# A four-layer graph network on one core: the load rearranged, and layer 1's sums moved between the blocks of a scan

## The reference, cut to what matters

```
x = layernorm(x + L0(x))
#  L0: deg = max(sum(adj,1)+1, 1); h = (adj @ x + x)/deg
#      z = relu([x, h] @ W + b);  z / max(|z|, 1e-12)
x = layernorm(x + L1(x))
#  L1: tanh([x, t] @ W1 + b1) @ W2 + b2 + adj @ (x B') - deg * (x B')
x = layernorm(x + L2(x))
#  L2: w @ (x @ weight) + bias, where w[i,j] = adj[i,j] * 0.5^(number of
#      neighbours of row i right of j), kept for the last 100 neighbours
x = layernorm(x + L3(x))
#  L3: logmap(adj @ expmap(x)) @ kernel + bias
```

## Time and profile before

| what | value |
|---|---|
| median of 3 runs | 169.18 us (169.04 to 169.3) |
| the profiled execution | 167.48 us |
| its span in the profile | 165.2 us |
| PE busy | 128.9 us, 78% of the span |
| DVE busy | 107.6 us, 65% |
| ACT busy | 69.5 us, 42% |
| POOL busy | 42.8 us, 26% |
| moved from memory | 17.93 MB |

### The profile page before, as it was taken

The page is one execution under the profiler, slowest core; times in us unless marked ns, Lnnn a source line. Parts: engine busy times, 40 slices in busy tenths (PEclk is TensorE's granted clock), DMA queues, the critical chain, the costliest instruction groups (busy, mean ns, idle before and its releaser), DMA issues.

```text
span 165.2 us, 2074 instructions
## 1 busy us (share of the span) xinstructions
PE 128.9 (78%) x728; PEld 67.7 (41%) x728; DVE 107.6 (65%) x240; ACT 69.5 (42%) x138; POOL 42.8 (26%) x50
## 2 busy tenths in 40 slices
PE   0018869957998899899999899999999899992000
PEld 0007753511443245143533555677447644572000
DVE  0589987789999999995176110622623888538861
ACT  0034201448566666754378547512113320257440
POOL 0000000102430143114344000433412552713290
PEclk9999999999999999999999999999999999999755
DMA  6999999999999995000000000000000000000006
GB/s 131 257 304 350 318 300 354 272 206 287 346 347 255 289 215 124 0 0 0 4 0 0 0 0 0 4 0 0 0 4 0 0 2 0 0 4 0 0 0 127
DMA packets 13945, 18.59 MB, mean 112 GB/s; under 512 B 5360, under 2 KB 5616, under 8 KB 13936
## 3 DMA queue, kind: packets, MB, share of 16 engines
q1 hardware_dynamic: 7728, 9.68, 22.2%
q10 hardware_dynamic: 6208, 8.78, 19.2%
HBM read 17.93 MB, written 0.52 MB: 112 GB/s over the span
## 4 chain that ended last, share of the span: by engine, by line
PE 45%; DVE 25%; DMA 13%; POOL 5%; issue 4%; ACT 4%; POOLq 1%; ACTq 0%; DVEq 0%
PE psS L737 15%; DMA WT<-adj 10%; PE psN L737 5%; PE psC L737 5%; DVE AT L494 4%; DVE AT L495 4%; DMA X<-x 3%; PE psC L804 3%; PE psC L806 3%; PE psX L813 2%; POOL root L272 2%; POOL nroot L291 2%; ACT WT L365 2%; PE psX L763 1%; PE psH L783 1%
## 5 line engine op out<-in xcount | busy, mean ns | idle before, releaser
L365 ACT ACTIVATE WT<-psC 128x512 int16<-128x512 f32 x64 | 36.9, 596 | 13.0 <-PE psC L806 9.8
L737 PE MATMUL psS<-AT,XP 128*128 128x512 bf16 x128 | 35.0, 390 | 0.9 <-DVE XP L500 0.9
L272 POOL TENSOR_TENSOR root<-var,power 128x4 f32<-128x4 f32 (+1 forms) x16 | 18.7, 1170 | 44.2 <-DVE var L546 19.5
L804 PE MATMUL psC<-AT,cb 128*128 128x512 bf16 x56 | 21.4, 383 | 4.5 <-ACT WT L365 4.5
L806 PE MATMUL psC<-AT,cb 128*128 128x512 bf16 x64 | 24.2, 379 | 0.0
L737 PEld LDWEIGHTS psS<-AT,XP 128*128 128x128 f16 x128 | 11.9, 100 | 17.0 <-issue 3.7
L763 PE MATMUL psX<-cb,XP 128*128 128x128 bf16 x32 | 4.0, 264 | 12.7 <-DVE XP L632 11.9
L494 DVE STREAM_TRANSPOSE AT<-stage 128x1024 bf16<-128x1024 bf16 x10 | 13.2, 1318 | 0.8 <-DMA stage<-adj 0.7
L804 PEld LDWEIGHTS psC<-AT,cb 128*128 128x128 bf16 x56 | 5.6, 101 | 18.6 <-ACT WT L365 16.0
L495 DVE STREAM_TRANSPOSE AT<-stage 128x1024 bf16<-128x1024 bf16 x10 | 12.7, 1270 | 0.0
L285 POOL TENSOR_TENSOR XB<-X,weights 128x256 f32<-128x256 f32 x12 | 9.6, 808 | 9.6 <-DVE X L551 9.6
(11 more groups left out here) (143 smaller groups left out, 223.3 us busy)
## 6 DMA issues: line engine op xcount, KB each, us to landing
stage<-adj ACTq DMA_DIRECT2D x20, 256.0 KB, 11.3
stage<-adj SPq DMA_DIRECT2D x20, 256.0 KB, 12.3
WT<-adj SPq DMA_DIRECT2D x12, 256.0 KB, 14.7
WT<-adj ACTq DMA_DIRECT2D x12, 256.0 KB, 14.0
out<-X SPq DMA_DIRECT2D x6, 64.0 KB, 1.9
weights<-weights_packed SPq DMA_DIRECT2D x1, 353.5 KB, 15.8
X<-x SPq DMA_DIRECT2D x2, 128.0 KB, 3.1
X<-x ACTq DMA_DIRECT2D x2, 128.0 KB, 4.0
```

The costliest lines, as they stand in the source:

```text
L272: nc.gpsimd.tensor_tensor(root[:, e, 0:n], var[:, e, 0:n], power[:, 0:n, 0:NR], ALU.pow).then_inc(root_ready, 1)
L365: nc.scalar.activation(WT[:, e, chain_block(bank, k)], psC[bank][:], ACT.Relu).then_inc(chain_taken, 1)
L737: ins = nc.tensor.matmul(bank, XP[:, l % 2, c], matrix, start=(c == 0), stop=last)
L804: nc.tensor.matmul(acc, C("past"), AT[:, c + 1, e], start=False, stop=False, skip_group_check=True)
```

## The change

On the load side:
- SP and ScalarE issue piece 0 before X. ScalarE issues pieces 1 to 5 at once, and later pieces at other places of its queue.
- VectorE transposes piece 0 before it waits for X, and piece 1 before it waits for the maximum. The high part of X's split moves to ScalarE (`split_high`).
- The parts of Z get four banks (psN[0], psN[1], psS[1], psC[0]); ScalarE takes them out, POOL adds the bias (`add_bias`).
- Chunk 0 is counted and summed in two halves of 256 columns: the first after pieces 0 and 1, ahead of the own parts, the second after them.
- VectorE's order from piece 6 on is written out; the last three transposes stand together ahead of activate0(2), and the centring of the weights moves behind it.

On the layer 1 side:
- CHAIN_IN_SUMS becomes (0, 10, 27, 38), CHAIN_LOOP 46. Eight sum blocks of layer 1 stand between chain blocks 18 to 25; transpose and hidden of chunk 0 stand among blocks 35 to 37, those of chunk 1 among 40 to 42.
- The last 18 chain blocks go in pairs between the steps of layer 1's end. POOL's residual additions of layer 1 come later in its queue.

```diff
 # SP
+            first = WR["WB"][0]
+            load_lower(0)
             for q in range(NQ // 2):
                 sp.dma_start(X[QD * q:QD * (q + 1)], xd[q]).then_inc(x_loaded, 16)
             sp.dma_start(cb[:].bitcast(U16), cpack).then_inc(consts_loaded, 16)
-            load_lower(0)
 # POOL
+            def add_bias(e):
+                pool.wait_ge(z_taken, e + 1)
+                nc.gpsimd.tensor_tensor(Z[:, chunk(e)], Z[:, chunk(e)], per_feature(W("b0")), ALU.add
+                                        ).then_inc(z_biased, 1)
 # ScalarE
+            def split_high():
+                act.wait_ge(inverse_ready, 1)
+                nc.scalar.activation(XP[:, 0, :, 0:D], X[:], ACT.Copy, scale=xs[:, 4:5]).then_inc(high_ready, 1)
+            def take_z(e):
+                act.wait_ge(z_ready, e + 1)
+                nc.scalar.activation(Z[:, chunk(e)], z_bank(e)[:, 0:NR * D]..., ACT.Copy).then_inc(z_taken, 1)
+            load_upper(0)
             for q in range(NQ // 2, NQ):
                 act.dma_start(X[QD * q:QD * (q + 1)], xd[q]).then_inc(x_loaded, 16)
-            for m in range(NR):
+            for m in range(1, 6):
                 load_upper(m)
-            for e in range(NE):
-                take_xt(0, e)
-                load_upper(NR + e)
+            split_high()
+            take_xt(0, 0)
+            load_upper(6)
+            take_xt(0, 1)
+            load_upper(7)
+            take_z(0)
+            take_xt(0, 2)
+            load_upper(8)
+            take_z(1)
+            take_xt(0, 3)
+            load_upper(9)
+            take_z(2)
+            take_z(3)
+            load_upper(10)
...
 # VectorE
+            transposes(0)
             dve.wait_ge(x_loaded, 16 * NQ)
             nc.vector.tensor_reduce(xs[:, 0:1], ...).then_inc(xmax_ready, 1)
             step(nc.vector.tensor_reduce(xmean[:], X[:], AX_X, ALU.add))
+            transposes(1)
             dve.wait_ge(xmax_all, 1)
...
-            transposes(0)
+            nc.vector.reciprocal(xs[:, 4:5], xs[:, 3:4]).then_inc(inverse_ready, 1)
             nc.vector.scalar_tensor_tensor(XB[:], per_node(xmean[:]), -1.0 / D, X[:], ALU.mult, ALU.add)
+            dve.wait_ge(high_ready, 1)
+            ... low part ...
+            for m in range(2, 6):
+                transposes(m)
+            ... h_bias ...
+            take_degrees(0); transposes(6); activate0(0); transposes(7); combine0(0)
+            transposes(8); normalise(0, 0); transposes(9); take_degrees(1); transposes(10)
+            activate0(1); transposes(11); combine0(1); transposes(12); normalise(0, 1)
+            take_degrees(2); transposes(13); transposes(14); transposes(15); activate0(2)
+            ... centring of the weights ...
+            take_degrees(3); combine0(2); activate0(3); normalise(0, 2); combine0(3); normalise(0, 3)
 # TensorE
+            count_half(0)
             transpose_x(0, 0)
+            sum_half(0)
+            transpose_x(0, 1)
+            own_part(0)
+            transpose_x(0, 2)
+            own_part(1)
+            transpose_x(0, 3)
+            own_part(2)
+            own_part(3)
+            count_half(1)
+            sum_half(1)
...
+                for k, n in enumerate(chain_after_sums(e)):
                     chain(n)
+                    if e == 1 and 2 <= k < 10:
+                        sum_block(1, k % 2, (k - 2) // 2)
...
+            chain_pair(CHAIN_LOOP)
             transpose_x(1, 2)
             sums(1, 1, late)
             add_own(1, 1)
+            chain_pair(CHAIN_LOOP + 2)
             dense(1, 0)
+            chain_pair(CHAIN_LOOP + 4)
             hidden(2)
+            sums(1, 2, late); add_own(1, 2); chain_pair(52); dense(1, 1); chain_pair(54)
+            transpose_x(1, 3); chain_pair(56); dense(1, 2); chain_pair(58); hidden(3)
+            chain_pair(60); chain_pair(62); sums(1, 3, range(0, 4)); add_own(1, 3)
```

More of the change, by code:

```diff
@@ L411, in _ @@
                 if e >= 1 and e < 3:
-                    for n in range(CHAIN_IN_SUMS[e], NB * e):
+                    for n in chain_in_sums(e):
                         take_chain(n)
+                        if n == CHAIN_IN_SUMS[1] + 4:
+                            load_upper(14)
                 take_sum(0, e)
                 if e < 3:
-                    for n in range(NB * e, CHAIN_IN_SUMS[e + 1]):
+                    for n in chain_after_sums(e):
                         take_chain(n)
[L418 to L423, removed]
@@ L646, in _ @@
                                            ).then_inc(h_bias_ready, 1)
+            take_degrees(0)
+            transposes(6)
+            activate0(0)
+            transposes(7)
+            combine0(0)
+            transposes(8)
+            normalise(0, 0)
+            transposes(9)
+            take_degrees(1)
+            transposes(10)
+            activate0(1)
+            transposes(11)
+            combine0(1)
+            transposes(12)
+            normalise(0, 1)
+            take_degrees(2)
+            transposes(13)
+            transposes(14)
+            transposes(15)
+            activate0(2)
             bundle = W(CENTRED[0], CENTRED[-1]).rearrange("p (k f) -> p k f", f=D)
@@ L650, in _ @@
                                            bundle, ALU.mult, ALU.add).then_inc(centred, 1)
[L651 to L657, removed]
-                activate0(e)
-                transposes(NR * e + 7)
-                combine0(e)
-            normalise(0, NE - 2)
-            take_degrees(NE - 1)
-            activate0(NE - 1)
-            combine0(NE - 1)
-            normalise(0, NE - 1)
+            take_degrees(3)
+            combine0(2)
+            activate0(3)
+            normalise(0, 2)
+            combine0(3)
+            normalise(0, 3)
             add_residual(1, 0)
@@ L807, in chain, with chain_pair @@
                                  skip_group_check=(k > 0)).then_inc(chain_ready, 1)
+            def chain_pair(n):
+                chain(n)
+                chain(n + 1)
             def hidden(e):
@@ L893, in _ @@
                 chain(n)
-                k = n - CHAIN_IN_SUMS[e] - 2
-                if k == -1:
+                k = n - CHAIN_IN_SUMS[e]
+                if k == 1:
                     dense(0, e)
-                if 0 <= k < 8:
+                if k == 2:
+                    transpose_x(1, 1)
+                if k == 4:
+                    hidden(1)
+                if k < 4:
+                    sum_block(1, 0, NR + k)
                     sum_block(1, 1, NR + k)
-                if 8 <= k < 12:
-                    sum_block(1, 0, k)
+            for c in range(2 * NR):
+                sum_block(1, 2, c)
+            for o in range(3):
+                sums(1, o, range(2, 3))
             sums(1, 0, late)
             add_own(1, 0)
+            chain_pair(CHAIN_LOOP)
             transpose_x(1, 2)
@@ L905, in _ @@
             add_own(1, 1)
+            chain_pair(CHAIN_LOOP + 2)
             dense(1, 0)
+            chain_pair(CHAIN_LOOP + 4)
             hidden(2)
-            for n in range(CHAIN_LOOP, CHAIN_ALL):
-                chain(n)
-                k = 2 * (n - CHAIN_LOOP)
-                if k < 12:
-                    sum_block(1, 2, k)
-                    sum_block(1, 2, k + 1)
-            dense(1, 1)
-            transpose_x(1, 3)
             sums(1, 2, late)
             add_own(1, 2)
-            sums(1, 3, range(0, 2))
+            chain_pair(CHAIN_LOOP + 6)
+            dense(1, 1)
+            chain_pair(CHAIN_LOOP + 8)
+            transpose_x(1, 3)
+            chain_pair(CHAIN_LOOP + 10)
+            dense(1, 2)
+            chain_pair(CHAIN_LOOP + 12)
             hidden(3)
-            dense(1, 2)
-            sums(1, 3, range(2, 4))
+            chain_pair(CHAIN_LOOP + 14)
+            chain_pair(CHAIN_LOOP + 16)
+            sums(1, 3, range(0, 4))
             add_own(1, 3)
```

169 lines of the change are left out of this document (103 added, 66 removed).

## The result

The changed kernel takes **167.03 us** (median of 4 runs, 166.16 to 167.45) against 169.24 us for the kernel before beside it (4 runs, 169.04 to 170.88): ratio 0.989, 95% interval 0.984 to 0.994. It is faster by 2.2 us where 2.4 slower was forecast. A second set of 12 runs gave 166.99 us, ratio 0.988 (0.984 to 0.992). The ratios leave disturbed runs out, so they can differ a little from the quotient of the medians.

What follows compares the result with a forecast made beforehand. VectorE was taken to set the pace, or nearly, up to 73 us, then TensorE. Layer 1's end at 115.0 against 112.08, less 0.5, gave +2.4: 169.9 profiled, 171.6 us as median; own range 170.3 to 172.8, over all cases 165.9 to 173.0.

Steps and rivals of the forecast that it cites:

- the 0.5 taken off: End of the sum: 0.5 us subtracted for a possible clock rise within the second half of chunk 0's sums.
- The start: Load up to TensorE's first transpose of X: piece 1, landing at 15.0, delays it to 20.7 us from 11.94.
- the table load: ScalarE's 1.28 us load before the high part: taken as hidden; a rival had it or the queue cost 1.3, chance 0.10.
- The clock: TensorE from 20.7 us: half sums and own parts at the low clock, own parts ending at 33.0, degrees at 35.9.
- The wait at take_degrees(0): VectorE ahead of piece 6: stands 5.8 us for the degrees of chunk 0; piece 7 ends at 45.3.
- early-clock rival: Start of TensorE's work: clock rises at 24.8, all after piece 7 is 5.8 earlier, 166.3 us; chance 0.32.
- The middle: VectorE from piece 7 to piece 15: 28.7 us, to 74.0; TensorE waits for piece 15, moved sums cost nothing.
- The end of layer 1: TensorE after chunk 3 of layer 0, from 78.9 us: 31.24 - 0.6 + 3.7 + 1.8, ending at 115.0 against 112.08.
- The stalls at the chain: Layer 1's end: new TensorE waits for ScalarE, 0.5 after hidden(1) and 1.3 at the last pairs and sums(1,3).
- No wait any more: Layer 1's end: split of chunk 3 comes 15 us after piece 15, at 89, needed at 90.9; 0.6 taken off.
- leftover work: After chunk 3 of layer 0: 4 chain blocks, 4 sums, a transpose and a hidden more remain, 3.7 us.
- From trace to median: Final step: the median's 1.7 us above the profiled execution is carried over, 169.9 to 171.6 us.

Runs made afterwards that it cites:

- half_late: The changed kernel with the first half of chunk 0's sums moved behind the own parts: 171.6 us, ratio 1.017.
- the two issue-time kernels: The kernel before and the changed kernel, each issuing upper halves of pieces 8 to 15 at the other's places: 168.11 us (0.994) and 168.68 us (0.995).
- layer1_only: The kernel before with only the change's chain and layer 1 orders on TensorE and ScalarE, load as before: 174.95 us, ratio 1.026.
- before_warm: The kernel before with twelve unused matmuls of 512 columns ahead of the first transpose of X: 169.67 us, ratio 1.007.
- before_early: The kernel before with upper halves of pieces 8 to 15 issued at the changed kernel's places: 168.11 us, ratio 0.994.
- load_only: The changed kernel's load with its VectorE and POOL orders, layer 1's blocks where they were before: 171.14 us, ratio 1.018.

## Why the prediction was wrong

The forecast, 171.6 us, was 4.6 too long. 2.7 of that lies in the trace (169.9 against 167.19) and 1.9 in the step from the profiled execution to the median. In the trace chunk 3 was over 4.2 us before the forecast, the end of layer 1 took 1.3 longer, and the 0.5 taken off was not to be had: layer 1's last block came at 112.10 instead of 114.5.

**The start: right in kind, late by 1.2.** X came at 11.60 instead of 9, outside the bound of 10.8, but at no cost, since piece 1 set the time: 16.29 instead of 15.0. The high part took 1.15 (0.96 estimated), the table load was hidden (8.79 us). The first transpose of X came at 21.92, forecast 20.7.

**The clock: the step that failed.** "At the low clock that the rows of before have for everything of this kind". The half sums end at 25.8, and from there everything ran at 2.4 GHz: the own parts ended at 30.35, not 33.0, and degrees were there at 32.2 instead of 35.9. half_late shows that the place of the half sums alone decides this: with the low clock its chunk 3 starts at 74.18, 4.3 us behind the changed kernel's 69.89. So up to there the forecast's sum fits the case that it had assumed (74.1), though a start 1.0 us later and a shorter wait (4.14 for 5.8) offset in it. The chances were wrong as well as the value. The rule of the Trainium skill (TensorE: Matmul & The Clock Gate, "The HAM clock gate"), that sustained activity releases the throttle, spoke for this rival, and the trace of the changed kernel agrees (2.4 GHz from about 25.7 us). The rows that the prediction held against it were of another kind: the 64-column f32 own parts, which half_late again shows at the low clock throughout (1.91 and 1.92 us, from 23.47 to 31 us), and the 4.8 us from the first counts to the rise, counts and sums that followed an idle time of 1.21 us.

**The wait at take_degrees(0): gone with it.** 5.8 us forecast, none measured. Piece 7 was done at 41.23: 4.1 before the forecast, 1.7 behind the early-clock rival's 39.5, of which 1.2 is the late start; the rest is put down to the waits for pieces 4 and 5 (1.56 us), partly covered.

**The middle: right.** From piece 7 to piece 15 28.5 us against 28.7 worked out, and TensorE waited for piece 15 (0.36 us), with the eight moved sums filling its gaps. Chunk 3 was over at 74.66, forecast 78.9.

**The end of layer 1: too short by 1.3.** From the end of chunk 3's sums to the last block 37.4 us passed, the forecast had 36.1. The stalls at the chain were nearly right (0.40 + 0.40 + 0.78 = 1.6, against 1.8). "No wait any more" for the split of chunk 3 was wrong: 0.84 us. The split was done 17.9 us after piece 15 and not 15: VectorE's operations of 0.43, 0.29 and 0.43 us took 1.28, 1.01 and 0.83 at 77.85, 81.06 and 82.11, beside POOL's work, and it waited 1.13 for POOL at 85.98. The wait that the forecast took off the kernel before was 0.43 and not 0.6, and TensorE's busy time came out 0.5 longer than 30.81 and the 3.7 of leftover work. This is why the trace shows nothing of the 2.9 us that the early-clock rival had: 6.2 us earlier at chunk 3, minus 3.7 of leftover work, 2.4 of waits where there had been 0.4, and the 0.5. Of those 6.2, moreover, only 3.1 are VectorE's: in the kernel before piece 15 was done at 72.95 and TensorE came to chunk 3 3.1 us later, busy with work that the change puts behind it. So VectorE set the pace only nearly up to 73 us, as the prediction allowed. The 0.5 us taken off for a rise within the second half of the sums had no counterpart.

**From trace to median: the second failure.** "I carry the difference over": the profiled execution of before was 1.7 below its median, so it was one of the best, while that of after is 0.2 above its own. The difference belongs to the execution and, as the two issue-time kernels show for about half of it, to something that the change removes; the rest stays open. The early-clock rival's 166.3 missed by 0.7 only because two errors offset: 2.6 too little in the trace (164.6 against 167.19), and 1.9 too much carried over.

## What to carry to other kernels

Put the densest matmuls that are ready ahead of small, slow ones at the start: here the order of the same instructions was worth 4.6 us through the clock. An engine freed early gives back what it gained unless the work that follows keeps up: read the waits of every later stage again, and price VectorE beside POOL. And look at whether a gain could lie in the spread between executions: a profiled execution that is one of the fastest may show fewer waits for transfers than most.

## What the runs showed of the hardware

- Up to the first rise of the clock the column of the granted clock read 1.00 (in half_late from 22 to 31 us, in before from 11 to 26), though the lengths there are those of 1.2 GHz. After it the column followed the lengths: 0.50 from 74 to 80 us in layer1_only, 0.50 from 22 to 30 in before_warm.
- After waits of TensorE of 3.96 and 2.30 us the same matmuls took nearly twice as long. After one of 1.51 an own part still took 1.08 (before_warm), after one of 1.59 the counts took 1.50 instead of 1.05 (before_early). After one of 3.05 us the low clock came late (load_only), TensorE:

```profile
88.82 0.39 PE L791 MATMUL psN<-AT,XP 128*128 128x512 bf16 x1 [3.05 <-DVE XP L552]
...
89.98 0.63 PE L880 MATMUL psC<-AT,cb 128*128 128x512 bf16 x1
```

- POOL's maximum over partitions ended between 8.0 and 11.0 us in the six traces with the load of before that have it, though its operand was ready at 6.3 to 7.4; in before_warm alone it began straight behind its operand.
- In the sixteen traces 137 of VectorE's operations on 128x256 took over 0.1 us more than usual, up to 1.28 for 0.43, and each lay beside one of POOL's on 256 or 512 elements per partition. Beside POOL's powers of 128x4 none did (343). Not every operation suffered: reductions took 0.42 at most. VectorE (first) and POOL of the changed kernel:

```profile
77.85 1.28 DVE L579 TENSOR_TENSOR u<-y 128x256 f32<-128x256 f32 x1
```
```profile
77.81 1.04 POOL L292 TENSOR_TENSOR diag<-cb,ndeg 128x512 f16<-128x512 bf16 x1
```

- Eight transfers behind ten others held ScalarE's queue for 10.87 us, and its next compute instruction stood behind them; the four in that place of the changed kernel took 2.11.
